# Recurrent layers: which engine scales the first norm, and at which place in its order

## The chip, the cores and the metric

The kernel runs on one core of a Trainium2 chip. The time is that of one execution on the device, in microseconds; a kernel's time is the median of its runs.

## The reference

Four layers work on x of 16 sequences by 100 tokens by 512 features, in fp32: a grouped-query attention (L0), a recurrent layer (L1), an attention with an MLP (L2), and a second recurrent layer of the same form (L3). The change touches L1 and L3 alone. Cut to what matters, such a layer computes:

```
xa = _ln(x, ln1_w, ln1_b)
sx = jnp.concatenate([state[:, 1:2] - xa[:, :1], xa[:, :-1] - xa[:, 1:]], axis=1)
xxx = jnp.tanh((xa + sx * maa_x) @ maa_w1).reshape(b, l, 5, DM)
xxx = jnp.einsum('blfd,fde->blfe', xxx, maa_w2)
xm = xa[:, :, None] + sx[:, :, None] * (maa_stack + xxx)
xk, xw, xv, xr, xg = (xm[:, :, j] for j in range(5))
...
def step(s, rkvw):
    r_t, k_t, v_t, w_t = rkvw
    a = k_t[..., :, None] * v_t[..., None, :]
    out = jnp.einsum('bhi,bhij->bhj', r_t, u * a + s)
    s = a + w_t[..., :, None] * s
    return (s, out)
...
og = ((og - m) / jnp.sqrt(va + 1e-05)).reshape(b, l, e) * gn_w + gn_b
x1 = x + og * g @ Wo.T
xc = _ln(x1, ln2_w, ln2_b)
...
return x1 + rr * (kk @ Wfv.T)
```

## The kernel before

Features lie on the 128 partitions in four chunks. A recurrent layer works through eight groups g = 0 to 7 of two sequences (200 columns). One pass of `body` does the recurrence of group g, the second half of group g - 1, the last gating of group g - 2 and the preparation of group g + 1 side by side. Its flags say which of these there are: `front` (prepare g + 1), `rec` (recurrence), `back` and `tail`. `turns` calls it for g = -1 (front alone, called the lead-in here), 0 (front, rec), 1 (front, rec, back), in a hardware loop for g = 2 to 6 (all four), and for 7 to 9 without front.

The recurrence runs over 16 items, each a slice of the state. For each item DVE multiplies keys and values (`product`, L708: two inputs from SBUF, the result to PSUM), then scans along time (`scan`, L723: decay from SBUF, products from PSUM). POOL multiplies the scanned states by r (L1107), and TensorE sums that over partitions (`reduce`, L500). Each engine has an order written by hand and waits for the others by semaphores. Between the items DVE does the other elementwise work; in `step(n)` stand product and scan of item n together.

The waits around the change:

- The first norm: TensorE's mean, DVE's centring (L243), ACT's square (L247), TensorE's variance (L252), ACT's logarithm and exponential (L258, L261), then `scale` (L266), the centred values times the reciprocal deviation, in place. It waits for `rstd`.
- ACT waits for the scale (`wait_scaled`) in its segment of item 5, then writes the affine result `xs` (L963). Behind it in ACT's order stand, when there is a group behind, the logarithm (L969) and exponential (L971) of the head norm, then the evictions of k and r (L978, L983), in the following segments those of v (L925) and the gate.
- DVE multiplies the head outputs by the head norm's result (L788, `head_normed`) after item 4, and later forms `sx` (L800) and `xx` (L804), the gated output (L812) and, after item 7, the bonus term (L823).
- TensorE's first token mix (L523) waits for that bonus; L509 is its projection of half a matrix, L516 and L237 its small sums.
- L782 is the last gating with the residual, between the items 3 and 4 of DVE, only with `tail`.
- In POOL's loop the product of item n waits for DVE's product n + 1:

```
wait(pool, "states", i, n + 1)
if n < 15:
    wait(pool, "kv", i, n + 2)
elif front:
    wait(pool, "kv", f, 1)
```

- At items 8 to 11 and 13 POOL also adds the token (L1087) ahead of its product.

Of the kernel before, what the change touches and what calls it, by code (L numbers as in the profile page):

```python
# [160 lines left out]
def two(v):  # L161

    return v.rearrange("p (a b) n -> p a (b n)", a=2)
# [228 lines left out]
def rwkv(core, m, name, base, after):  # L392
# [7 lines left out]
    def wait(eng, n, i, k=0):  # L400

        eng.wait_ge(m.s[n].sem, m.s[n].at(i, k))

    def sem(n):
        return m.s[n].sem
# [5 lines left out]
    def seq(v):  # L411
        return v.rearrange("p c (b t) -> p c b t", b=NB)

    def pairs(v, cc):

        return v[:, 2 * cc:2 * cc + 2, :].rearrange("p c (b t) -> p (c b) t", b=NB)
# [56 lines left out]
    def turns(eng, body):  # L473

        core.wait_before(eng, after)
        wait(eng, "weights", occ + 1)
        body(base - 1, -1, front=True, rec=False, back=False, tail=False)
        wait(eng, "weights_back", occ + 1)
        body(base, 0, front=True, rec=True, back=False, tail=False)
        body(base + 1, 1, front=True, rec=True, back=True, tail=False)  # L480
        with eng.Fori(2, G - 1) as g:
            body(g + base, g, front=True, rec=True, back=True, tail=True)
        body(base + G - 1, G - 1, front=False, rec=True, back=True, tail=True)
        body(base + G, G, front=False, rec=False, back=True, tail=True)
        body(base + G + 1, G + 1, front=False, rec=False, back=False, tail=True)
# [200 lines left out]
    def vector(dve):  # L686
        def body(i, g, front, rec, back, tail):
            f, b, t = i + 1, i - 1, i - 2
# [81 lines left out]
            if back:  # L770
# [2 lines left out]
                wait(dve, "head_out", b, 2)  # L773
                wait(dve, "head_mean", b, 1)
                dve.tensor_tensor(two(m.oc), two(m.bon), wide[2], ALU.subtract).then_inc(sem("head_centred"), 1)
            if front:
                m.n1.scale(dve, f)

            step(3)
            if tail:  # L780
# [115 lines left out]
        dve.memset(m.k.rearrange("p c b e -> p (c b) e")[:, :, 0:1], 1.0).then_inc(sem("columns"), 1)  # L896
        dve.memset(m.v.rearrange("p c b e -> p (c b) e")[:, :, 0:1], 0.0).then_inc(sem("columns"), 1)
        turns(dve, body)


# [180 lines left out]
    def gpsimd(pool):  # L1081
        def body(i, g, front, rec, back, tail):
            f = i + 1

            def add_token(x):
                wait(pool, "mix_term", f, 4 * x + 4)
                pool.tensor_tensor(seq(m.xm[x]), seq(m.xm[x]), m.xs[:, :, :, 1:E], ALU.add).then_inc(sem("mixed"), 1)  # L1087

            for n in range(16):
                if rec:  # L1090
                    if n % 8 == 0:
                        wait(pool, "r", i, n // 8 + 1)
                    sv = m.ring[n % 4].rearrange("p (h c) (b e) -> p h (c b) e", h=2, b=NB)[:, :, :, 0:L]
                    rb = pairs(m.r, n // 8).unsqueeze(1).broadcast_to([P, 2, 2 * NB, L])
# [5 lines that stand above are left out]
                if front and 8 <= n < 12:  # L1100
                    add_token(n - 8)
                if front and n == 13:
                    add_token(4)
                if rec:
                    if n == 13:
                        wait(pool, "kv", i, 16)
                    pool.tensor_tensor(sv, sv, rb, ALU.mult).then_inc(sem("r_states"), 1)  # L1107

        turns(pool, body)
# [1213 lines left out]
```

## Time and profile before

| | us |
|---|---|
| median of 3 runs | 3081.06 (3078.34 to 3083.32) |
| profiled execution | 3076.93 |
| its span, first to last instruction | 3075.0 |
| busy: TensorE (PE) | 2811.2 |
| busy: VectorE (DVE) | 2003.5 |
| busy: ScalarE (ACT) | 1350.9 |
| busy: GpSimd (POOL) | 665.0 |

The shares are of the whole span, attention layers included. L1 runs from about 636 to 1300 us, L3 from about 2365 to the end. A row of a timeline gives start and busy time in us, engine, line, operation, what it writes and reads, how many such instructions are merged (x4), and in brackets the idle time ahead and what ended it. An instruction can start up to 0.1 us before its forerunner has ended.

### The profile page before, as it was taken

The numbers are of one execution on the slowest core, as the hardware profiler recorded it, in microseconds if no ns is written. First come the engines' busy times: TensorE is split into PE (matmuls) and PEld (weight loads), VectorE is DVE, ScalarE is ACT, GpSimd is POOL, SyncE is SP. The second block draws the span as 40 slices with busy tenths as digits, with TensorE's granted clock in tenths as the row PEclk, the third lists the DMA queues.
The fourth block names the chain that finished last, engine by engine and source line by source line (L and its number), as shares of the span: only waits on it lengthen the run. The fifth ranks groups of instructions, "written<-read, shape, count | busy, mean of one in ns | idle before, by whom it ended". The sixth has DMA issues, their size and how long they took to land.

```text
span 3075.0 us, 53764 instructions
## 1 busy us (share of the span) xinstructions
PE 2811.2 (91%) x18112; PEld 2186.9 (71%) x18112; DVE 2003.5 (65%) x4888; ACT 1350.9 (44%) x3446; POOL 665.0 (22%) x436
## 2 busy tenths in 40 slices
PE   7999999967999999779999999999997889999986
PEld 7555555856888888666555455799996768888866
DVE  2878787338999999644555556511101699999993
ACT  1888888542443443343444444332311234444432
POOL 0111110015444444300000000000000454444440
PEclk9999999978999999889999999999998899999998
DMA  2100100313333333300000000300002333333340
GB/s 107 36 24 34 34 23 13 130 41 98 92 92 90 88 91 92 107 27 10 30 20 19 26 22 10 126 26 1 0 1 89 92 95 92 89 92 92 87 126 14
DMA packets 96167, 182.85 MB, mean 59 GB/s; under 512 B 10122, under 2 KB 87498, under 8 KB 92462
## 3 DMA queue, kind: packets, MB, share of 16 engines
q1 hardware_dynamic: 96046, 181.27, 19.2%
q8 instruction: 72, 1.18, 0.2%
q14 instruction: 49, 0.40, 0.0%
HBM read 171.34 MB, written 9.90 MB: 59 GB/s over the span
## 4 chain that ended last, share of the span: by engine, by line
PE 66%; DVE 12%; issue 9%; ACT 8%; DMA 2%; POOL 1%; SPq 0%; DVEq 0%; ACTq 0%; POOLq 0%
PE psum L509 19%; PE psum L314 10%; PE psum L1859 6%; PE psum L1746 4%; PE psum L1303 3%; DVE psum L708 3%; PE psum L500 3%; ACT arena L1506 3%; ACT arena L2126 2%; PE psum L1759 2%; PE psum L1801 2%; PE psum L516 2%; PE psum L1315 2%; DVE arena L723 2%; PE psum L523 2%
## 5 line engine op out<-in xcount | busy, mean ns | idle before, releaser
L509 PE MATMUL psum<-arena 128*128 128x200 f32 x4096 | 772.1, 347 | 51.5 <-DVE arena L876 18.6
L509 PEld LDWEIGHTS psum<-arena 128*128 128x128 f32 x4096 | 721.9, 198 | 135.6 <-issue 79.3
L1107 POOL TENSOR_TENSOR arena<-arena 128x800 f32<-128x800 f32 x256 | 454.9, 1780 | 452.2 <-DVE psum L708 452.2
L723 DVE TENSOR_TENSOR_SCAN arena<-arena,psum 128x808 f32<-128x808 f32 x256 | 470.0, 1836 | 37.3 <-PE psum L500 22.1
L314 PE MATMUL psum<-arena 128*128 128x200 f32 (+1 forms) x1920 | 332.1, 335 | 15.0 <-POOLq L139 13.3
L314 PEld LDWEIGHTS psum<-arena 128*128 128x128 f32 x1920 | 328.5, 192 | 16.7 <-POOLq L139 13.3
L1506 ACT ACTIVATE arena<-arena 100x361 f32<-100x361 f32 x512 | 300.6, 590 | 87.2 <-DVE arena L1417 85.5
L1087 POOL TENSOR_TENSOR arena<-arena 128x800 f32<-128x800 f32 x80 | 140.6, 1757 | 807.6 <-DVE arena L731 632.3
L708 DVE TENSOR_TENSOR psum<-arena 128x808 f32<-128x808 f32 x256 | 280.6, 1096 | 5.5
L1417 DVE CUSTOM_DVE_ANT_0 arena<-psum,arena 100x361 f32<-100x361 f32 x512 | 254.3, 531 | 45.4 <-ACT arena L1506 37.9
L1303 PEld LDWEIGHTS psum<-arena 100*128 100x128 f32 x1536 | 146.3, 142 | 131.2 <-ACT arena L1518 60.3
L2126 ACT ACTIVATE arena<-arena 100x361 f32<-100x361 f32 x256 | 149.6, 587 | 146.5 <-DVE arena L1999 146.5
L1303 PE MATMUL psum<-arena 100*128 100x100 f32 x1536 | 189.5, 258 | 24.3 <-ACT arena L1518 24.1
L1801 PEld LDWEIGHTS psum<-arena 100*128 100x128 f32 x768 | 84.5, 141 | 148.8 <-issue 74.8
L1759 PE MATMUL psum<-arena 128*128 128x512 f32 (+1 forms) x384 | 189.4, 605 | 0.0
L1746 PE MATMUL psum<-arena 128*128 128x361 f32 x512 | 180.2, 477 | 1.6 <-DVE arena L1927 1.5
L1859 PE MATMUL psum<-arena 128*128 128x200 f32 x1024 | 175.0, 333 | 0.1
L1859 PEld LDWEIGHTS psum<-arena 128*128 128x128 f32 x1024 | 173.4, 190 | 0.4 <-DMA arena<-L_fc 0.4
L914 ACT ACTIVATE arena<-arena 128x8 f32 (+1 forms) x256 | 54.1, 212 | 267.7 <-DMA arena<-v_rows 266.7
L247 ACT ACTIVATE arena<-arena 128x800 f32<-128x800 f32 x56 | 48.7, 870 | 262.3 <-DVE arena L243 262.1
L731 DVE SCALAR_TENSOR_TENSOR arena<-psum,arena 128x200 f32<-128x200 f32 x320 | 112.9, 415 | 57.8 <-PE psum L523 57.8
L500 PE MATMUL psum<-arena 128*32 128x400 f32 x1024 | 127.6, 537 | 23.8 <-POOL arena L1107 14.2
(142 smaller groups left out, 3908.3 us busy)
## 6 DMA issues: line engine op xcount, KB each, us to landing
arena<-v_rows SPq DMA_DIRECT2D x512, 202.0 KB, 3.2
arena<-ctxT SPq DMA_DIRECT2D x32, 722.0 KB, 4.2
arena<-L_w SPq DMA_DIRECT2D x9, 1024.0 KB, 10.5
arena<-L_w SPq DMA_DIRECT2D x8, 1152.0 KB, 16.1
v_rows<-arena SPq DMA_DIRECT2D x32, 202.0 KB, 2.1
arena<-L_fc SPq DMA_DIRECT2D x4, 1024.0 KB, 8.3
arena<-L_pj SPq DMA_DIRECT2D x4, 1024.0 KB, 15.5
arena<-xT SPq DMA_DIRECT2D x4, 800.0 KB, 12.0
```

The source lines that it names most:

```text
L314: mm = pe.matmul(core.part(w, m), weight[:, k, m * P:(m + 1) * P], src(k), start=k == 0, stop=k == k_chunks - 1)
L500: mm = pe.matmul(psum[r0:r0 + 32, 6, 0:2 * N], core.red_w[:, 24 - 8 * q:56 - 8 * q], rv[:, h, :, 0:L], start=q == 0, stop=q == 3)
L509: mm = pe.matmul(chunk(bank, j), m.W[n][:, k, c * P:(c + 1) * P], src[:, k, :], start=k == 0, stop=k == C - 1)
L708: dve.tensor_tensor(m.kv.rearrange("p (h x) -> p h x", h=2), kb, m.spread[n % 4].rearrange("p h a e -> p h (a e)"), ALU.mult).then_inc(sem ...
L723: dve.tensor_tensor_scan(m.ring[n % 4].rearrange("p j e -> p (j e)"), m.we[:, cc].rearrange("p j e -> p (j e)"), m.kv, 0.0, ALU.mult, ALU. ...
L1107: pool.tensor_tensor(sv, sv, rb, ALU.mult).then_inc(sem("r_states"), 1)
L1303: mm = pe.transpose(bank[4 + 3 * (n % 2)][:, j * L:(j + 1) * L], pr[h % 8][0:L, j * P:(j + 1) * P], ident[0:L, 0:L])
L1417: dve.tensor_tensor_reduce(out=sm[n][0:L], in0=bank[n][0:L, 0:S], in1=nmask[u][0:L], scale=1.0, scalar=FLT, op0=ALU.add, op1=ALU.min, accu ...
L1506: act.activation(pr[k % 8][0:L, 0:S], sm[n][0:L], ACT.Exp, bias=nmx[0:L, k:k + 1], scale=-1.0, accum_out=den[0:L, k:k + 1]).then_inc(exp_r ...
L1746: mm = pe.matmul(bank[6 + c % 2][:, 0:S], Wk[:, k, c * P:(c + 1) * P], ctxt[u % 2][:, k, :], start=k == 0, stop=k == C - 1)
L1759: mm = pe.matmul(bank[6 + j % 2][0:n, :], ctxt[u % 2][:, k, a:a + n], Wv[:, k, :], start=k == 0, stop=k == C - 1)
L1859: mm = pe.matmul(part(2 + q % 2, m), fc[:, k, j * P:(j + 1) * P], norms[u].yc[:, k, :], start=k == 0, stop=k == C - 1)
```

## The change

The call of the scale leaves DVE's order, where it stood after the head centring and before item 3, and enters POOL's, ahead of the product of item 3. The wait for `rstd` goes with it. Nothing else is edited.

```diff
@@ -773,8 +773,6 @@
                 wait(dve, "head_out", b, 2)
                 wait(dve, "head_mean", b, 1)
                 dve.tensor_tensor(two(m.oc), two(m.bon), wide[2], ALU.subtract).then_inc(sem("head_centred"), 1)
-            if front:
-                m.n1.scale(dve, f)
 
             step(3)
             if tail:
@@ -1087,6 +1085,8 @@
                 pool.tensor_tensor(seq(m.xm[x]), seq(m.xm[x]), m.xs[:, :, :, 1:E], ALU.add).then_inc(sem("mixed"), 1)
 
             for n in range(16):
+                if front and n == 3:
+                    m.n1.scale(pool, f)
                 if rec:
                     if n % 8 == 0:
                         wait(pool, "r", i, n // 8 + 1)
```

POOL's order in the loop of L1, from item 1 to item 4, before the change (L402 is the helper that waits, L1107 the product):

```order
L1107 TENSOR_TENSOR arena<-arena 128x8x100
L402 REGISTER_ALU
L1107 TENSOR_TENSOR arena<-arena 128x8x100
L402 REGISTER_ALU
L1107 TENSOR_TENSOR arena<-arena 128x8x100
L402 REGISTER_ALU
L1107 TENSOR_TENSOR arena<-arena 128x8x100
```

The same place after it:

```order
L1107 TENSOR_TENSOR arena<-arena 128x8x100
L402 REGISTER_ALU
L1107 TENSOR_TENSOR arena<-arena 128x8x100
L264 REGISTER_ALU
L266 TENSOR_TENSOR arena<-arena 128x800
L402 REGISTER_ALU
L1107 TENSOR_TENSOR arena<-arena 128x8x100
L402 REGISTER_ALU
```

The scale stands between the products of items 2 and 3, with a register instruction for its wait ahead.

DVE's order in the loop of L1, from the head centring (L775) over the product (L708) and scan (L723) of item 3 to the last gating (L782), before the change:

```order
L775 TENSOR_TENSOR arena<-arena,psum 128x800
L266 TENSOR_TENSOR arena<-arena 128x800
L402 REGISTER_ALU
L708 TENSOR_TENSOR psum<-arena 128x808
L723 SCALAR_TENSOR_TENSOR arena<-arena,psum 128x808
L782 ISA
L782 SCALAR_TENSOR_TENSOR arena<-arena 128x4x200
```

The same place after it (lines below the edit have moved up by two, 775 is 773 and so on):

```order
L775 TENSOR_TENSOR arena<-arena,psum 128x800
L402 REGISTER_ALU
L708 TENSOR_TENSOR psum<-arena 128x808
L723 SCALAR_TENSOR_TENSOR arena<-arena,psum 128x808
L780 ISA
L780 SCALAR_TENSOR_TENSOR arena<-arena 128x4x200
```

The scale is gone, and item 3 follows the head centring directly.

## Rows read from the trace of the kernel before

**Rows 1.** Windows view, one stretch of L1: us, then busy us (instructions) by engine, PEclk, DMA.

```profile
840.00:1160.00 320.00, 314.10 (x1838) 270.08 (x1838) 301.07 (x359) 136.35 (x284) 152.16 (x86) 0.98 0.32 89
```

**Rows 2.** Timeline, DVE, pass g = 6 of L1: start us, busy us, engine, line, operation.

```profile
1151.42 0.99 DVE L266 TENSOR_TENSOR arena<-arena 128x800 f32<-128x800 f32 x1
...
1152.32 1.00 DVE L708 TENSOR_TENSOR psum<-arena 128x808 f32<-128x808 f32 x1
...
1153.36 1.84 DVE L723 TENSOR_TENSOR_SCAN arena<-arena,psum 128x808 f32<-128x808 f32 x1
...
1155.12 0.97 DVE L782 SCALAR_TENSOR_TENSOR arena<-arena 128x800 f32 x1
...
1156.00 1.00 DVE L708 TENSOR_TENSOR psum<-arena 128x808 f32<-128x808 f32 x1
...
1159.02 0.99 DVE L788 TENSOR_TENSOR arena<-arena 128x800 f32<-128x800 f32 x1
```

**Rows 3.** Timeline, ACT, the same pass.

```profile
1152.53 1.89 ACT L963 ACTIVATE arena<-arena 128x200 f32<-128x200 f32 x4
...
1154.58 1.28 ACT L969 ACT_TABLE_LOAD   x1 [0.16 <-PE psum L516]
...
1158.12 0.87 ACT L971 ACTIVATE arena<-arena 128x800 f32<-128x800 f32 x1
```

**Rows 4.** Timeline, DVE, further on in the same pass.

```profile
1174.07 0.96 DVE L823 TENSOR_TENSOR arena<-psum,arena 128x800 f32<-128x800 f32 x1
...
1193.82 0.97 DVE L266 TENSOR_TENSOR arena<-arena 128x800 f32<-128x800 f32 x1
```

**Rows 5.** Timeline, TensorE products and weight loads, the same pass.

```profile
1152.95 1.52 PE L516 MATMUL psum<-arena 128*128 128x200 f32 x8
...
1175.08 1.31 PEld L523 LDWEIGHTS psum<-arena 32*128 32x128 f32 x8 [0.33 <-DVE arena L823]
...
1194.05 4.65 PE L509 MATMUL psum<-arena 128*128 128x200 f32 x16 [1.14 <-POOL arena L1087]
```

**Rows 6.** Timeline, POOL, product of item 2, the same pass.

```profile
1153.41 1.75 POOL L1107 TENSOR_TENSOR arena<-arena 128x800 f32<-128x800 f32 x1 [5.46 <-DVE psum L708]
```

**Rows 7.** Timeline, POOL, a pair without a pause, further on.

```profile
1192.19 1.73 POOL L1087 TENSOR_TENSOR arena<-arena 128x800 f32<-128x800 f32 x1 [1.02 <-DVE psum L708]
1193.88 2.52 POOL L1107 TENSOR_TENSOR arena<-arena 128x800 f32<-128x800 f32 x1
```

**Rows 8.** Timelines of POOL and DVE, end of pass g = 5 of L1.

```profile
1134.88 3.45 POOL L1107 TENSOR_TENSOR arena<-arena 128x800 f32<-128x800 f32 x2 [1.25 <-DVE psum L708]
...
1136.71 2.49 DVE L708 TENSOR_TENSOR psum<-arena 128x808 f32<-128x808 f32 x1
```

**Rows 9.** Timelines of POOL, ACT, DVE and TensorE, pass g = 1 of L1.

```profile
762.73 1.75 POOL L1107 TENSOR_TENSOR arena<-arena 128x800 f32<-128x800 f32 x1 [6.55 <-DVE psum L708]
...
761.70 1.89 ACT L963 ACTIVATE arena<-arena 128x200 f32<-128x200 f32 x4
...
783.01 0.96 DVE L823 TENSOR_TENSOR arena<-psum,arena 128x800 f32<-128x800 f32 x1
...
784.99 1.61 PE L523 MATMUL psum<-arena 32*128 32x200 f32 x8
```

**Rows 10.** Timeline, ACT, lead-in pass of L1.

```profile
643.50 1.89 ACT L963 ACTIVATE arena<-arena 128x200 f32<-128x200 f32 x4 [1.06 <-DVE arena L266]
```

**Rows 11.** Timelines: the pause of TensorE in pass g = 2; DVE's L266 in g = 2, 3, 5.

```profile
881.26 2.97 PE L509 MATMUL psum<-arena 128*128 128x200 f32 x16 [1.14 <-POOL arena L1087]
...
838.64 0.99 DVE L266 TENSOR_TENSOR arena<-arena 128x800 f32<-128x800 f32 x1
...
916.17 0.98 DVE L266 TENSOR_TENSOR arena<-arena 128x800 f32<-128x800 f32 x1
...
1072.99 0.99 DVE L266 TENSOR_TENSOR arena<-arena 128x800 f32<-128x800 f32 x1
```

**Rows 12.** Windows view, 2 us behind the pause of TensorE, pass g = 6; PEclk is third from last.

```profile
1196.00:1198.00 2.00, 2.00 (x7) 2.00 (x7) 1.52 (x3) 0.72 (x2) 0.72 (x2) 0.52 0.00 0
```

## Prediction

> **What bounds the kernel now.** Only the two recurrent layers (L1, L3) hold the edited lines, so I read their steady passes, first by the busy table, then by each engine's timeline, then by who waited for whom. From 840 to 1160, four of L1's five passes g = 2 to 6 ("steady" below; L3 has five as well), TensorE is busy 314 of 320 us and DVE 301 [rows 1]: TensorE is idle some 1.4 us of a pass of 78, DVE 4.6. So the question is not how busy DVE is, but whether the moved step lies on a path that reaches TensorE late.
>
> Follow one steady pass. DVE does the scale (L266) at 1151.42, item 3's product at 1152.32, its scan at 1153.36, the residual (L782) at 1155.12, item 4's product at 1156.00, and the head scaling (L788) at 1159.02 [rows 2]. ACT is what the scale feeds: the affine L963 starts at 1152.53, 0.12 after the scale's end at 1152.41; a table load for the head norm's logarithm follows at 1154.58, and the exponential L971 ends at 1158.12 + 0.87 = 1158.99 [rows 3]. DVE's L788 starts 0.03 later. Its scan of item 4 is over by then too, so both arrive together: **L788 has no slack against ACT**. From there DVE works without a pause to L823 at 1174.07, ended 1175.03 [rows 4], and TensorE's token mix (the first of the five) starts at 1175.08, its weight load having idled 0.33 until L823 [rows 5]. Such loads idle 0.24 in other places for nothing but issue, so TensorE was ready some 0.1 before DVE. The chain scale, L963, L971, L788, L823, mix is therefore critical in a steady pass, and the same 0.32 to 0.34 stands before that mix in all ten steady passes. A delay of the scale's end moves the whole following pass.
>
> **The change, part by part.**
> *DVE loses the scale.* Its slot is 1152.32 − 1151.42 = 0.90 [rows 2]. Item 3's product starts at 1151.42 instead, its scan at 1152.46, L782 would at 1154.22.
>
> *POOL gains it, behind product 2.* That product cannot start before DVE has multiplied item 3: it starts at 1153.41 now, 0.05 behind the scan [rows 6], so at 1152.51 then. A POOL instruction that follows another directly starts 1193.88 − 1192.19 = 1.69 later [rows 7], and an undisturbed one of this size takes 1.75 [rows 6]. So the scale would start at 1154.20 and end at 1155.95, against 1152.41: **3.54 later**. Only 0.75 of this is POOL's slower arithmetic (1.75 against 0.99 for 800 elements of a partition); the rest is the place in POOL's order. Queued behind the scale on POOL stands product 3, which waits for DVE's product 4 anyway; on ACT, behind L963, stand the head norm and the evictions of the keys and of r, late by as much.
>
> *Who gets SBUF first.* Rows show that POOL and a DVE instruction with two SBUF inputs do not run together. DVE's L266 started at 1193.82, POOL's product 0.06 later, and took 2.52 instead of 1.75 [rows 4, 7]; where POOL's second product began about 0.13 ahead (1134.88 + 1.70), DVE's product at 1136.71 took 2.49 instead of 1.00 [rows 8]. In the steady pass the scale (1154.20) meets L782 (1154.22), which reads two SBUF tensors: a tie. If POOL wins, the scale ends at 1155.95, L782 and product 4 run behind it, and the scan of item 4 is over by about 1159.7, still before ACT lets L788 go. If DVE wins, POOL waits until L782 has read: 2.52 − 1.75 = 0.77 behind its own start at the row of 1193.88, about 0.84 behind DVE's; the scale runs 1155.06 to 1156.81, **4.40 later**. If it also waited for product 4 (0.88 more), 5.3. In the loop POOL has a register instruction between product 2 and the scale; POOL's lead of 0.02 is less than anything such a step can cost, so I take DVE first, 4.40, and keep 3.54 and 5.3 as ends.
> The Trainium skill, SBUF — State Buffer, section "SBUF: two separate sides", says the pair is an exclusive lock for whichever starts first, held for the whole instruction. Taken by start times alone it would hand the tie to POOL, and the sum below would be 41 instead of 50. By that rule, the two collisions above agree with it, and no row of before shows a tie as close as this.
>
> *What reaches TensorE.* ACT's table load now waits also for TensorE's variance product, ended at 1154.47 [rows 3, 5], so 0.14 of the delay is absorbed: L788 and L823 are late by 3.40 or 4.26 (4.26 at DVE first). Ten steady passes: 34.0 or 42.6 us.
>
> *Passes g = 1 (two).* No residual there, DVE's next product comes later than the scale, so POOL is first: product 2 at 762.73 − 0.90 = 761.83, scale 763.52 to 765.27, L963 at 765.39 instead of 761.70 [rows 9]: 3.7 late, with nothing to absorb it at the table load. But L823 ends at 783.97 and the mix starts at 784.99 [rows 9], so 1.0 is hidden: 2.7 each, 5.4.
>
> *Passes g = 0 (two).* There is no head norm to pass through ACT, and DVE wants the result only after three more products. What is left is DVE's next product shut out by the scale, at most 1.75 less the 0.90 that DVE saves: between 0 and 0.85 each, taken as 0. *The lead-in (two)*: the scale stands in a bare chain, L963 idling 1.06 for it [rows 10], its 0.99 and a hop; POOL's 1.75 for 0.99 gives 0.76, and a hop no shorter, so 0.8 each, 1.6.
>
> *TensorE's clock.* In the pass read above, the pause of 1.14 before L509 at 1194.05 was followed by 16 products in 4.65 [rows 5]; the same pause at 881.26 by 2.97 [rows 11]. From 1196 to 1198, behind that pause, the granted clock reads 0.52 [rows 12], near the lower of its two levels (1.2 GHz; 1.00 is 2.4). So after such a pause the clock sometimes falls, and 1.68 is lost. The slow kind came in four of five steady passes of each layer. The passes with it are 1151.42 − 1072.99 = 78.43 long, one without it 916.17 − 838.64 = 77.53 [rows 2, 11]: 0.9 net. After the change TensorE pauses a second time, some 2 us before the mix. Bounds: 0, and 12 x 1.68 = 20. I take half of the twelve at 0.9: 5.4.
>
> **Sum:** 42.6 + 5.4 + 0 + 1.6 + 5.4 = 55. The profiled execution took 3076.93 (span 3075.0); the median of the runs is 3081.06, 4 above it, and the difference is added to that: **3136 us**, 1.8% slower.
>
> **Rivals.**
> *POOL wins the tie* (slower, less): 34.0 + 5.4 + 1.6 = 41, with the clock term 46: 3122 to 3127. For it: the start times; against it: the register step.
> *The wait grows* (slower, more): 5.3 − 0.14 = 5.16 a pass gives 51.6 + 7.0 = 59, or the clock falls in every pass: 42.6 + 7.0 + 20 = 70; 3140 to 3151. Against the first: POOL asks before product 4 does.
> *TensorE hides it* (no change): if the true bound were TensorE's own work and the 0.33 before the mix were mere issue, passes would lose only the lead-in's 1.6: 3083. Against it: that row names L823, and 1.4 us idle in a pass cannot hide 3.4.
> *DVE is relieved* (faster): the place is DVE's slot between L775 and product 3. If the recurrence of products and scans on DVE set the pass, and ACT could take L963 after the head norm, 14 slots of 0.90 would come back: 3081 − 12.6 = 3068. It decides if L788 starts earlier than 1159.02 less 0.9, for which ACT would need more than 4 us of slack; it has 0.03.
> *It does not do what it says*: POOL's order shows the scale behind product 2, and DVE's lacks it. No chance given.
>
> **How the numbers follow.** Forecast (DVE first, clock term between its bounds) 0.48; POOL first 0.30; wait grows or clock in all 0.11; hidden 0.06; faster 0.05. The range 3114 to 3153 takes in the first three with their bounds, and a loss one fifth smaller than POOL first gives, since not all slack behind L788 is seen; it leaves out hidden and faster, and some of the tails. A measurement of this kernel tells about 0.2%, 6 us, from no change. Slower by over 0.2%: 0.89; within: 0.06; faster: 0.05.
>
> **What would show it.** L266 on POOL, 1.75 or about 2.5 long (the tie), ending 3.5 to 4.4 later behind the scan of item 3 than now; L788 idle about 3 us until ACT's L971; L823 late, and a weight load of the mix idle 2 us or more; steady passes 81 to 83 instead of 77.5 to 78.4. Wrong if L788 shows no wait for ACT, or if passes keep their length.

## The result, and the profile after

The changed kernel takes 3130.46 us (median of four runs, 3129.18 to 3135.71), the kernel before 3082.19 in four runs beside it (3078.34 to 3084.07): ratio 1.0161, interval 1.0144 to 1.0179. It is slower by 48 us. The profiled executions stand 52.4 apart (spans 3127.4 and 3075.0). Lines below the first edit moved up by two: L782 is L780 now, L788 L786, L823 L821, L963 L961, L971 L969, L978 L976, L1087 L1085; L775 and all lines above the first edit keep their numbers, in the listing of DVE's order as well.

The page of the changed kernel, costliest groups: busy time, mean ns of one, then the idle time ahead and what ended most of it.

```profile
L509 PE MATMUL psum<-arena 128*128 128x200 f32 x4096 | 759.6, 343 | 90.5 <-ACT arena L976 23.6
...
L708 DVE TENSOR_TENSOR psum<-arena 128x808 f32<-128x808 f32 x256 | 303.5, 1186 | 5.7
...
L266 POOL TENSOR_TENSOR arena<-arena 128x800 f32<-128x800 f32 x16 | 38.4, 2397 | 571.3 <-ACT arena L261 571.3
```

The same groups of TensorE and of DVE's products on the page of the kernel before, for the comparison:

```profile
L509 PE MATMUL psum<-arena 128*128 128x200 f32 x4096 | 772.1, 347 | 51.5 <-DVE arena L876 18.6
...
L708 DVE TENSOR_TENSOR psum<-arena 128x808 f32<-128x808 f32 x256 | 280.6, 1096 | 5.5
```

The sixteen scales are on POOL and take 2.4 us on average. DVE lost 16 scales of 0.99, but its products grew by 22.9 us altogether: what it was to be relieved of comes back as waiting inside its own instructions. TensorE's largest group is idle for 90.5 us, where it was 51.5, and the first cause named is ACT's L976, the eviction of the keys, which stands behind the head norm on ACT.

A steady pass of the changed kernel, g = 2 of L1. Timeline of POOL (start us, busy us, engine, line, operation, idle time ahead):

```profile
848.05 1.74 POOL L1107 TENSOR_TENSOR arena<-arena 128x800 f32<-128x800 f32 x1 [4.02 <-DVE psum L708]
849.75 2.71 POOL L266 TENSOR_TENSOR arena<-arena 128x800 f32<-128x800 f32 x1
853.41 1.74 POOL L1107 TENSOR_TENSOR arena<-arena 128x800 f32<-128x800 f32 x1 [0.94 <-DVE psum L708]
```

Timeline of DVE, the same pass:

```profile
848.01 1.84 DVE L723 TENSOR_TENSOR_SCAN arena<-arena,psum 128x808 f32<-128x808 f32 x1
...
849.76 0.97 DVE L780 SCALAR_TENSOR_TENSOR arena<-arena 128x800 f32 x1
850.64 2.69 DVE L708 TENSOR_TENSOR psum<-arena 128x808 f32<-128x808 f32 x1
...
858.93 0.99 DVE L786 TENSOR_TENSOR arena<-arena 128x800 f32<-128x800 f32 x1 [3.63 <-ACT arena L969]
...
873.97 0.96 DVE L821 TENSOR_TENSOR arena<-psum,arena 128x800 f32<-128x800 f32 x1
```

Timeline of ACT, the same pass:

```profile
852.59 1.89 ACT L961 ACTIVATE arena<-arena 128x200 f32<-128x200 f32 x4 [4.52 <-POOL arena L266]
...
858.03 0.87 ACT L969 ACTIVATE arena<-arena 128x800 f32<-128x800 f32 x1
```

Timeline of TensorE, products and weight loads, the same pass:

```profile
859.44 5.68 PE L509 MATMUL psum<-arena 128*128 128x200 f32 x32 [2.19 <-ACT arena L976]
...
871.41 2.94 PE L509 MATMUL psum<-arena 128*128 128x200 f32 x16 [1.18 <-DVE arena L745]
...
874.99 1.31 PEld L523 LDWEIGHTS psum<-arena 32*128 32x128 f32 x8 [0.94 <-DVE arena L821]
...
893.94 2.97 PE L509 MATMUL psum<-arena 128*128 128x200 f32 x16 [1.13 <-POOL arena L1085]
```

What to see here. The scale starts 1.70 behind product 2, as a POOL pair does in [rows 7]. DVE's residual L780 starts at the same moment, is through in its ordinary 0.97, and POOL takes 2.71: DVE was served first. The scale ends at 852.46, 4.45 behind the start of item 3's scan. ACT's affine waits for it (4.52), the exponential L969 ends at 858.90, and DVE's L786 starts 0.03 later, after 3.63 idle. In [rows 2, 3] the same 0.03 stood there without an idle time ahead. From L786 to L821 it is 15.04 us, before it was 15.05 [rows 2, 4], and the mix follows L821 by 1.02, before by 1.01 [rows 4, 5]. So the delay travels unchanged to TensorE.

The steady passes, from one head centring of DVE to the next, are 81.85 to 81.91 us long in eight cases of ten (before 77.53 to 77.57 without and 78.4 with a fall of the clock; g = 6 is shorter in both kernels). Two neighbouring head centrings on DVE's timeline:

```profile
846.07 0.99 DVE L775 TENSOR_TENSOR arena<-arena,psum 128x800 f32<-128x800 f32 x1 [0.69 <-PE psum L516]
...
927.92 0.99 DVE L775 TENSOR_TENSOR arena<-arena,psum 128x800 f32<-128x800 f32 x1 [0.69 <-PE psum L516]
```

The windows view of the changed kernel, the stretch of [rows 1]:

```profile
840.00:1160.00 320.00, 297.35 (x1750) 252.09 (x1748) 293.42 (x343) 125.38 (x265) 154.90 (x86) 1.00 0.30 86
```

TensorE is busy 297 of 320 us instead of 314, and its granted clock reads 1.00 instead of 0.98. In the last TensorE row above the pause of 1.13 is followed by products at full speed (2.97); in [rows 5] the same pause was followed by 4.65. Such falls came in eight of the ten steady passes before, and in none of the ten now.

### The profile page after: what moved, and what is told of

The parts are those of the page before. It is cut to its first block, busy times and chain, and to the rows that moved or that the text cites. A ratio compares the mean times of both kernels' runs of the same rounds, so it can differ in the third digit from the quotient of the medians.

```text
span 3127.4 us, 53774 instructions
## 1 busy us (share of the span) xinstructions
PE 2811.1 (90%) x18112; PEld 2177.9 (70%) x18112; DVE 2021.0 (65%) x4872; ACT 1346.6 (43%) x3446; POOL 702.0 (22%) x452
## 3 DMA queue, kind: packets, MB, share of 16 engines
q8 instruction: 72, 1.18, 0.2%
## 4 chain that ended last, share of the span: by engine, by line
PE 52%; DVE 18%; issue 13%; ACT 10%; POOL 3%; DMA 2%; DVEq 1%; ACTq 0%; SPq 0%; POOLq 0%
PE psum L314 10%; PE psum L509 10%; PE psum L1859 6%; PE psum L1746 4%; DVE psum L708 4%; PE psum L1303 3%; DVE arena L723 3%; ACT arena L1506 2%; ACT arena L2126 2%; PE psum L1759 2%; PE psum L1801 2%; PE psum L1315 2%; DVE arena L731 2%; PE psum L1282 2%; PE psum L500 2%
## 5 line engine op out<-in xcount | busy, mean ns | idle before, releaser
L509 PE MATMUL psum<-arena 128*128 128x200 f32 x4096 | 759.6, 343 | 90.5 <-ACT arena L976 23.6
L509 PEld LDWEIGHTS psum<-arena 128*128 128x128 f32 x4096 | 709.9, 195 | 176.9 <-issue 84.8
L1107 POOL TENSOR_TENSOR arena<-arena 128x800 f32<-128x800 f32 x256 | 454.3, 1777 | 468.5 <-DVE psum L708 468.5
L723 DVE TENSOR_TENSOR_SCAN arena<-arena,psum 128x808 f32<-128x808 f32 x256 | 469.9, 1835 | 25.4 <-PE psum L500 10.1
L708 DVE TENSOR_TENSOR psum<-arena 128x808 f32<-128x808 f32 x256 | 303.5, 1186 | 5.7
L1085 POOL TENSOR_TENSOR arena<-arena 128x800 f32<-128x800 f32 x80 | 140.4, 1755 | 233.3 <-DVE psum L708 174.7
L1859 PE MATMUL psum<-arena 128*128 128x200 f32 x1024 | 175.0, 333 | 0.0
L266 POOL TENSOR_TENSOR arena<-arena 128x800 f32<-128x800 f32 x16 | 38.4, 2397 | 571.3 <-ACT arena L261 571.3
L523 PE MATMUL psum<-arena 32*128 32x200 f32 x640 | 133.8, 349 | 22.3 <-DVE arena L821 11.7
```

The source lines that it names most:

```text
L509: mm = pe.matmul(chunk(bank, j), m.W[n][:, k, c * P:(c + 1) * P], src[:, k, :], start=k == 0, stop=k == C - 1)
L708: dve.tensor_tensor(m.kv.rearrange("p (h x) -> p h x", h=2), kb, m.spread[n % 4].rearrange("p h a e -> p h (a e)"), ALU.mult).then_inc(sem ...
L723: dve.tensor_tensor_scan(m.ring[n % 4].rearrange("p j e -> p (j e)"), m.we[:, cc].rearrange("p j e -> p (j e)"), m.kv, 0.0, ALU.mult, ALU. ...
L1859: mm = pe.matmul(part(2 + q % 2, m), fc[:, k, j * P:(j + 1) * P], norms[u].yc[:, k, :], start=k == 0, stop=k == C - 1)
```

## The experiments

Besides the theory on record (what is late is the scale's place, then the tie for SBUF), these rivals were open: that POOL's work as such costs the time, that DVE's freed slot gives something back, and that a contest elsewhere decides. The kernel before ran beside them, 19 times for the first four (median 3082.05) and 19 times for the last three (3082.2).

### The scale stays on DVE, but late

Kernel before, with the scale put behind item 3 on DVE:

```diff
-            if front:
-                m.n1.scale(dve, f)
 
             step(3)
+            if front:
+                m.n1.scale(dve, f)
```

> The kernel before, with the scale still on DVE but behind the scan of item 3 instead of ahead of its product: no POOL, no collision in SBUF, only a later result. Theory (the loss is the lateness of the scale's end, carried by ACT's affine and head norm to DVE's head scaling and to TensorE's mix): the scale ends about 2.8 us later, 2.66 of it arrive in each of ten steady passes and 1.8 in each pass g = 1, some of it given back where TensorE's clock falls less often (0.9 in up to eight passes): 3104 to 3112 us, steady passes about 80.2, the head scaling idle for ACT about 2 us. Rival (the loss is POOL's slower instruction and its collision with DVE): nothing is left of it, within 4 us of before, 3078 to 3086.

Measured: 3107.29 (3104.54 to 3111.80), ratio 1.0078, interval 1.0061 to 1.0095. Timeline of DVE in that kernel, a steady pass:

```profile
1086.59 1.84 DVE L723 TENSOR_TENSOR_SCAN arena<-arena,psum 128x808 f32<-128x808 f32 x1
1088.35 0.97 DVE L266 TENSOR_TENSOR arena<-arena 128x800 f32<-128x800 f32 x1
...
1095.78 0.99 DVE L788 TENSOR_TENSOR arena<-arena 128x800 f32<-128x800 f32 x1 [2.67 <-ACT arena L971]
```

Nothing is on POOL, nothing is slower, and DVE's sum of work is the same. The scale ends at 1089.32, 2.73 behind the scan's start instead of 0.95 ahead of it [rows 2]; 0.90 of that difference of 3.68 is the scan's own earlier start, so it is 2.78 late. L788 waits 2.67 for ACT, and a pass without a fall of the clock is 80.14 instead of 77.53: 2.61 more. **Lateness alone costs 2.61 a pass**, and the rival that only work on POOL costs time is out.

### One place earlier on POOL

Changed kernel, with the scale ahead of POOL's product 2:

```diff
-                if front and n == 3:
+                if front and n == 2:
```

> The changed kernel, with the scale on POOL one item earlier, ahead of the product of item 2, where POOL idles and the reciprocal deviation is ready (in the pass read before, from about 1148.9 to 1150.8, against 1152.41 for DVE's). Theory: the result is not late, so the whole loss goes: 3078 to 3085 us; no gain over before, since ACT's head norm waits for TensorE's variance product then and still ends at the same place. Rival (POOL's instruction itself and its hold on SBUF cost 4 us a pass): it stays slower than 3110.

Measured: 3083.70 (3076.70 to 3086.19, ten runs), ratio 1.0004, interval 0.9994 to 1.0013: the whole loss is gone, and there is no gain. POOL in that kernel, then DVE, one steady pass:

```profile
1070.59 1.89 POOL L266 TENSOR_TENSOR arena<-arena 128x800 f32<-128x800 f32 x1 [0.97 <-ACT arena L261]
```

```profile
1072.19 0.99 DVE L775 TENSOR_TENSOR arena<-arena,psum 128x800 f32<-128x800 f32 x1 [0.78 <-PE psum L516]
1073.10 1.00 DVE L708 TENSOR_TENSOR psum<-arena 128x808 f32<-128x808 f32 x1
...
1080.69 0.99 DVE L786 TENSOR_TENSOR arena<-arena 128x800 f32<-128x800 f32 x1 [0.95 <-ACT arena L969]
```

POOL starts the scale as soon as ACT's `rstd` is there, ahead of DVE's head centring, which waits for TensorE, and is done at 1072.48. DVE saves its slot of 0.90 and then waits 0.95 for ACT. This is the "DVE is relieved" rival tried under its best conditions: the pass stays at 77.5 and 78.4 us. From the head centring to L786 it is 8.50, as it was to L788 before: ACT's head norm goes through the square of the centred outputs and TensorE's variance product, and ends no sooner.

### The residual moved away from the tie

Changed kernel, with the residual (L780) put behind item 4:

```diff
             step(3)
+
+            step(4)
             if tail:
                 wait(dve, "ffn_gated", t, 2)
...
-            step(4)
```

> The changed kernel, with DVE's last gating and residual moved from behind the scan of item 3 to behind the scan of item 4, into DVE's wait for ACT. It takes away the instruction that gets into SBUF ahead of POOL's scale. Theory (losing the tie costs POOL 0.84 us, and all of it reaches TensorE): the scale takes 1.87 instead of 2.71, ten passes are 0.84 shorter: 3122 us (3119 to 3125), steady passes 81.0. Rival (the collision is hidden by another wait): 3130 as the change.

Measured: 3124.45 (3121.03 to 3126.69), ratio 1.0139, interval 1.0122 to 1.0156. Timelines of POOL and of DVE in that kernel:

```profile
1089.05 1.89 POOL L266 TENSOR_TENSOR arena<-arena 128x800 f32<-128x800 f32 x1
```

```profile
1089.25 2.55 DVE L708 TENSOR_TENSOR psum<-arena 128x808 f32<-128x808 f32 x1
...
1097.40 0.99 DVE L787 TENSOR_TENSOR arena<-arena 128x800 f32<-128x800 f32 x1 [2.74 <-ACT arena L970]
```

DVE's next instruction with two SBUF inputs comes 0.20 behind the scale now, POOL is first, and the scale takes 1.89. A pass without a fall is 81.04: 3.51 over 77.53, where the changed kernel has 81.87, 4.34 over it. **The lost tie is 0.83 of it.** The edit also moves a piece of DVE's own work, into its wait for ACT, which is still 2.74 long. The clock fell again in eight of the ten steady passes, which takes most of it back: together the ten are only 2.2 us shorter than in the changed kernel. The medians are 6 us apart, and the rest of that comes from elsewhere, so the expected length of a pass (81.0) was met, and the expected total partly by luck. The first head centring of L1 alone comes 5.6 us earlier in this run (759.69 against 765.27).

### The head norm ahead of the affine on ACT

Changed kernel, with ACT's two blocks of that segment exchanged, so that the exponential no longer stands behind the affine that needs the scale:

```diff
             start(5)
-            if front:
-                m.n1.wait_scaled(act, f)
...
             if back:
                 wait(act, "head_var", b, 1)
...
                 act.activation(m.ors, m.ors, ACT.Exp, scale=-0.5).then_inc(sem("head_rstd"), 1)
+            if front:
+                m.n1.wait_scaled(act, f)
```

> The changed kernel, with ACT's affine of the first norm moved behind the head norm's logarithm and exponential in its order. The scale stays late on POOL, but the head scaling no longer depends on it. Theory (the road of the delay is ACT's order, in which the head norm stands behind the affine): what is left is DVE's product of item 4, shut out by the scale, which makes the head scaling some 0.7 us late: 3085 to 3093 us. Rival (the delay comes by the token shift and mix, which need the affine itself, or by DVE's collision): 3120 or more.

Measured: 3086.60 (3082.20 to 3092.37, ten runs), ratio 1.0016, interval 1.0006 to 1.0026. Timelines of POOL, ACT and DVE:

```profile
1075.61 2.71 POOL L266 TENSOR_TENSOR arena<-arena 128x800 f32<-128x800 f32 x1
```

```profile
1079.52 0.87 ACT L962 ACTIVATE arena<-arena 128x800 f32<-128x800 f32 x1
1080.30 1.88 ACT L968 ACTIVATE arena<-arena 128x200 f32<-128x200 f32 x4
```

```profile
1076.49 2.69 DVE L708 TENSOR_TENSOR psum<-arena 128x808 f32<-128x808 f32 x1
...
1081.08 0.97 DVE L786 TENSOR_TENSOR arena<-arena 128x800 f32<-128x800 f32 x1
```

The scale is as late and as slow as in the changed kernel (2.71, tie lost), and DVE's product is held up as long. But L786 has no idle time now, and of the 48 us some 44 are gone. Counted in passes without a fall, 3.7 of 4.34 are gone. This shows that the collision itself is not what costs most: the delay reaches TensorE because the head norm's exponential is queued behind the affine on ACT. The passes are 78.13 each, 0.6 over 77.53, and the clock fell in one of ten.

### A copy moved, to shorten DVE's part

The last three kernels ask whether DVE's work can be turned into time. The 8-element copy of the first state (L842 before), which takes 1.00 us behind the norm centring, is put right behind the residual that it does not depend on, in the kernel before, in the changed kernel, and in the one with the scale one place earlier:

```diff
                                   ALU.add).then_inc(sem("x1"), 1)
+                dve.tensor_copy(m.xs2[:, :, :, 0], core.st[:, :, 0, ds(g - 1, NB)]).then_inc(sem("state0_in_xs2"), 1)
...
                 m.n2.dve_center(dve, xg(g - 1), b)
-                dve.tensor_copy(m.xs2[:, :, :, 0], core.st[:, :, 0, ds(g - 1, NB)]).then_inc(sem("state0_in_xs2"), 1)
```

> The kernel before, with DVE's small copy of the second state column moved from behind the second norm's centring (where it took 1.00 instead of 0.15 us, shut out of SBUF by POOL's product) to behind the residual x1, where POOL idles. DVE is 0.85 us earlier on the stretch that ends in TensorE's pause of 1.14 before the projection of v, so the pause shrinks to about 0.3 and, if the clock falls because of it, the falls of 0.9 net in eight passes go: 12 x 0.85 + 8 x 0.9 = 17 us at most, 3065 to 3073 us, steady passes 76.7. If the pause is set by something else: 3080 to 3084.

> The changed kernel with the same copy moved. The profile of the changed kernel shows no fall of the clock in its ten steady passes, the one before eight. So here only the 0.85 a pass is won: 3130 - 10 = 3120 us (3117 to 3123), steady passes 81.0. Against the kernel before with the copy moved the change then costs 4.3 us in each steady pass without a refund by the clock: 50 us or more apart. If the falls of the clock had nothing to do with the pause, the two are 48 apart as the first pair.

> The scale on POOL ahead of the product of item 2, and the copy moved. The scale's place saves DVE 0.9 us where it then waits for ACT, which is worth nothing, so this stands within 4 us of the kernel before with the copy moved alone: 3065 to 3073 us, 0.3 to 0.5% faster than before. If DVE's 0.9 us were worth something: 3055 to 3062.

| kernel | measured us | ratio, interval |
|---|---|---|
| kernel before, copy moved | 3085.10 (3080.55 to 3093.24) | 1.0009 (0.9999 to 1.0018) |
| changed kernel, copy moved | 3140.50 (3138.03 to 3147.29) | 1.0192 (1.0170 to 1.0214) |
| one place earlier, copy moved | 3088.19 (3083.43 to 3093.26) | 1.0019 (1.0008 to 1.0029) |

All three missed their level. The kernel before with the copy moved, DVE, POOL and TensorE at the end of a pass:

```profile
1122.48 2.34 DVE L266 TENSOR_TENSOR arena<-arena 128x800 f32<-128x800 f32 x1 [0.23 <-ACT arena L261]
...
1129.43 2.57 DVE L870 TENSOR_TENSOR arena<-arena 128x800 f32<-128x800 f32 x1
```

```profile
1122.23 1.74 POOL L1107 TENSOR_TENSOR arena<-arena 128x800 f32<-128x800 f32 x1
...
1129.41 1.74 POOL L1107 TENSOR_TENSOR arena<-arena 128x800 f32<-128x800 f32 x1
```

```profile
1122.41 2.97 PE L509 MATMUL psum<-arena 128*128 128x200 f32 x16 [0.39 <-POOL arena L1087]
...
1129.51 2.98 PE L509 MATMUL psum<-arena 128*128 128x200 f32 x16 [1.20 <-POOL arena L1087]
```

The copy did shrink, to 0.16. But DVE and POOL now meet in another way: L266, which began 0.06 ahead of POOL in [rows 4, 7] and took 0.97, comes 0.25 behind it and takes 2.34, and L870 comes 0.02 behind and takes 2.57. L870 took 0.97 in the kernel before only in the eight passes with a fall of the clock; in the two without it had met POOL too. Timeline of DVE there, g = 2:

```profile
886.86 2.31 DVE L870 TENSOR_TENSOR arena<-arena 128x800 f32<-128x800 f32 x1
```

So against a pass without a fall 1.37 (L266) and 0.26 (L870) are new and 0.84 of the copy is saved: 0.79 of the 0.84 us by which the pass grew. TensorE's pause of 1.14 shrank to 0.39 and came back as 1.20 seven microseconds on. The passes are 78.37 each, longer than the 77.53 of a pass without a fall. The clock fell in two of the ten here, both g = 6, and in none of the ten in the third kernel. What the third kernel was for held: it is within 4 us of the first (3.1), so DVE's 0.90 is worth nothing in that company either. The second was 20 us slower than expected. Its steady passes without a fall are 82.5 (g = 2) and 82.7 to 82.8 long, about 0.9 over the changed kernel's where 0.85 less was expected: an estimated 17 of the 20 over ten passes, and the same growth as in the kernel before. The clock fell in three of ten; two of these passes are 83.8 long, 1.0 more each, and the third is g = 6, with 81.16 against 81.13 in the layer where it did not fall. Against the kernel before with the copy moved it is 55.4 slower, as expected (50 or more), and their passes without a fall stand 4.37 apart (4.34 in the first pair).

## Why the prediction was right, step by step

The forecast was 3136 against 3130.46, inside the range of 3114 to 3153, and slower as said. In the profiled executions the forecast of 55 stands against 52.4:

| term | forecast | measured |
|---|---|---|
| ten steady passes, without the clock | 42.6 | 43.4 |
| clock in the steady passes | +5.4 (all passes) | −6.1 |
| passes g = 1, two | 5.4 | 6.7 |
| L1 from its start to the first head centring (lead-in and g = 0) | 0.8 | 4.7 |
| the same stretch of L3 | 0.8 | −0.7 |
| passes behind the loop, two | 0 | 2.4 |
| elsewhere | 0 | 2.0 |

43.4 is ten times 81.87 − 77.53 = 4.34. −6.1 is what the measured 37.3 leaves, and eight vanished falls account for it: six of 0.9 and two, in g = 6, of 0.35, the difference that a fall makes to g = 6 with the scale late on DVE (78.87 with one, 78.52 without). The total lies nearer to the forecast than its terms do: the clock is 11.5 under its term, all others together are 8.9 over theirs. So part of that nearness is luck.

**The critical chain** (scale, affine, exponential, L788, L823, mix) was right. The experiment with the head norm first cuts it at one point and nearly all of the loss goes. The rival that TensorE hides it fell with it.

**The start of the scale** was right to 0.01: 1.74 behind the scan's start, forecast 1154.20 − 1152.46.

**The tie** was right in who is served first, and not for the reason given, so this hit is luck. I argued that the register step would make POOL late; it did not. POOL's record starts at 849.75 and DVE's at 849.76, and still POOL waited. The price was forecast from a collision as 0.86 between the two choices and measured as 0.83. The rule of the Trainium skill, SBUF — State Buffer, section "SBUF: two separate sides", that whoever starts first holds the lock, would have given 3.51 a pass by recorded starts. The runs gave that where POOL's lead was 0.20, and not in the tie. In between the recorded starts do not decide. In the three kernels with the copy moved POOL's L1107 leads DVE's L870 by about 0.02 in all thirty steady passes: POOL was first in 28, and DVE in two, both in the changed kernel. Its timelines of POOL and DVE (L870 is L868 there), first one of the two, then one of the others:

```profile
896.96 2.60 POOL L1107 TENSOR_TENSOR arena<-arena 128x800 f32<-128x800 f32 x1
896.98 0.97 DVE L868 TENSOR_TENSOR arena<-arena 128x800 f32<-128x800 f32 x1
...
979.46 1.74 POOL L1107 TENSOR_TENSOR arena<-arena 128x800 f32<-128x800 f32 x1
979.49 2.56 DVE L868 TENSOR_TENSOR arena<-arena 128x800 f32<-128x800 f32 x1
```

Whether the rule is off here, or the recorded start is not the moment that counts, is open.

**The duration on POOL** was mis-sized a little: 1.87 to 1.89 undisturbed, not the 1.75 of the product of the same size in [rows 6]. This is the term by which 4.34 came out over 4.26. Of the 4.34, 2.61 is the place in the order (the scale late on DVE), 0.90 POOL's slower instruction (3.51 − 2.61; 1.89 less 0.97), and 0.83 the lost tie (4.34 − 3.51).

**Passes g = 0**: DVE's product, 0.13 behind the scale, took 2.61 and 2.60 instead of 1.01. DVE saved the scale's slot and the 0.58 and 0.79 that it had idled for ACT ahead of it, so that DVE came out 0.2 later in L1 and no later in L3, against 0 forecast.

**Passes g = 1** came to 2.85 and 3.84 against 2.7 each; the longer scale (1.88) gives the first, the second is from L3, whose pass before was itself 0.7 shorter. **The lead-in**: ACT's wait there rose from 1.06 [rows 10] to 2.07, 1.0 each against 0.8, the longer scale again:

```profile
642.16 1.87 POOL L266 TENSOR_TENSOR arena<-arena 128x800 f32<-128x800 f32 x1 [93.53 <-ACT arena L261]
644.06 1.89 ACT L961 ACTIVATE arena<-arena 128x200 f32<-128x200 f32 x4 [2.07 <-POOL arena L266]
```

**The clock term had the wrong sign.** I had expected a second pause of TensorE to cost falls of the clock. The second pause came, and the falls behind the first one went: 6.1 us back instead of 5.4 lost. That is why the total came in under the forecast although each pass is longer than forecast. Behind the start of L1 the clock went both ways: TensorE's variance product of the lead-in took 1.77 instead of 3.04, but then 16 products took 5.70 instead of 4.59, and the pause of 1.17 is followed by 4.40 where one of 1.16 was followed by 2.97 before. Timeline of TensorE in the changed kernel, L1's lead-in and pass g = 0:

```profile
660.68 5.70 PE L509 MATMUL psum<-arena 128*128 128x200 f32 x16
...
732.05 4.40 PE L509 MATMUL psum<-arena 128*128 128x200 f32 x16 [1.17 <-POOL arena L1085]
```

Together with the lead-in this is the larger part of the 4.7 of that stretch. L3 runs the same instructions there and came out at −0.7; its 16 products of the lead-in took 4.42 where they took 5.70. What decides over such a fall is open: the falls in ten steady passes were 8 before, 0 after the change, 6 with the scale late on DVE, 7 one place earlier, 8 with the residual moved, 1 with the head norm first, 2, 3 and 0 with the copy moved, and the granted clock over the whole profiled run was between 0.958 and 0.965 in all of them.

**What the signs said.** I had asked for L788 idle about 3 (it was 3.63), passes of 81 to 83 (81.9), and a weight load of the mix idle 2 or more. The last was wrong: it idles 0.94, 0.61 more than in [rows 5]. The rest of the delay reaches TensorE earlier, in two pauses: 2.19 before the L509 at 859.44, which waits for L976, the eviction behind the same head norm, and 1.18 before the L509 at 871.41, which waits for DVE's L745. I had named that eviction as late, and not followed it to TensorE.

Open is also the 1.2 us by which each of the two passes behind the loop grew (64.48 and 64.67 to 65.65 and 65.89). With the scale late on DVE they are 65.64 and 66.13, so it does not take POOL.

## What to carry to other kernels

Before an operation moves to another engine, look at the instruction it will stand behind there and at the one that stands behind its reader: here the place in two in-order queues (POOL's, and ACT's with the exponential behind the affine) cost more than the slower instruction, and one place earlier, or ACT's two blocks exchanged, took nearly all of it back. Time freed on a busy engine is worth something only if its next input is there earlier as well: DVE's 0.90 turned into 0.95 of waiting.

## What the runs showed of the hardware

- **In this tie for SBUF DVE was first.** In all ten steady passes of the changed kernel the scale on POOL started 0.00 to 0.02 ahead of DVE's residual by the records and took 2.70 to 2.72, while DVE took 0.96 to 0.97; with the head norm first it was the same. POOL gets in right behind: DVE's next product, which starts 0.88 later, takes 2.68 to 2.69. It is no rule for every near tie: with another pair of instructions and about 0.02 of lead POOL was first in 28 passes of 30 (L870 at 1129.43 behind POOL's 1129.41 took 2.57).
- **An earlier DVE can be a slower one.** With its copy shortened by 0.84, DVE lost a contest that it had won (L266, 1.37 more) and, in the passes where it had not met POOL before, a second one (L870, 1.6 more). The pages count this as busy time of DVE.
- **The same instruction class differs on POOL**: 1.87 to 1.89 for the scale, 1.73 to 1.76 for the product of as many elements. On DVE the scale takes 0.97 to 0.99, and its own product of 808 elements 1.00. The scale's second operand is repeated over the four chunks of features, that of POOL's product over two halves; whether that is the reason was not tried.
- **A pause of TensorE of 1.12 to 1.15 us is followed by a fall of the clock in some passes and by none in others**, and 16 products take up to 4.65 instead of 2.97. Of these 1.68 about 0.9 reaches the length of a pass, and 0.35 in g = 6. This came in patterns that changed with every edit, also with edits that left the length of the pass alone.
